# Merging own and former scores into one row of 128 keys, and the first batch's scores from whole fp32 parts, in a transformer layer on one core

## The reference, cut to what matters

```python
x = x + attn(layernorm(x), qkv_w, out_w)      # 16 heads of 16, rotary on q and k, scale 16**-0.5
x = x + ffn(layernorm(x), w1, w2, h1, h2, w3) # silu(w1 x) * (w2 x), gelu(h1 .), gelu(h2 .), w3; hidden 1024

def block_mask(seq_len):                      # which key j a query i sees
    blk = i // 64 == j // 64
    glob = (i < 4) | (j < 4)
    slide = abs(i - j) <= 128
    return (blk | glob | slide) & (j <= i)
```

## Time and profile before

| | |
|---|---|
| median of 3 runs (lowest, highest) | 1135.43 us (1133.87, 1138.61) |
| the profiled execution's own time | 1138.62 us |
| its span, first to last instruction | 1136.8 us |
| TensorE (PE) busy | 1077.8 us, 95% |
| VectorE (DVE) | 638.8 us, 56% |
| ScalarE (ACT) | 717.5 us, 63% |
| GpSimd (POOL) | 473.4 us, 42% |
| mean granted TensorE clock | 0.973 |

### The profile page before, as it was taken

How to read it: one execution, slowest core, us unless ns; L and a number is a source line. 1 busy time by engine, 2 the same in 40 slices (tenths; PEclk the granted TensorE clock), 3 DMA queues, 4 the chain that set the end, 5 groups by cost and what they waited for, 6 DMA issues and landing times.

```text
span 1136.8 us, 21541 instructions
## 1 busy us (share of the span) xinstructions
PE 1077.8 (95%) x7538; PEld 887.7 (78%) x7538; DVE 638.8 (56%) x1986; ACT 717.5 (63%) x1774; POOL 473.4 (42%) x656
## 2 busy tenths in 40 slices
PE   4676899999999999999999999999999999999997
PEld 2455787879778897888878797788978888888886
DVE  4586457555665465654575556654656544555312
ACT  2555458585586576685585865865766855966422
...
GB/s 377 315 167 222 259 206 221 287 146 120 182 223 148 160 184 131 242 84 203 165 167 188 151 119 176 227 145 165 179 130 225 84 201 167 122 103 70 173 128 20
DMA packets 120380, 198.53 MB, mean 175 GB/s; under 512 B 7632, under 2 KB 71376, under 8 KB 119248
## 3 DMA queue, kind: packets, MB, share of 16 engines
...
q10 hardware_dynamic: 1152, 11.53, 2.6%
...
## 4 chain that ended last, share of the span: by engine, by line
PE 78%; ACT 9%; DVE 5%; POOL 3%; issue 3%; DMA 1%; SPq 0%; POOLq 0%; ACTq 0%; DVEq 0%
PE bank L731 35%; PE bank L701 11%; PE bank L755 4%; PE bank L592 4%; PE bank L635 4%; PE bank L529 4%; PE bank L604 3%; PE bank L612 3%; ACT Sm L887 3%; PE bank L557 2%; PE bank L660 2%; POOL a_lo L1370 2%; DVE Sm L1101 2%; ACT L907 2%; ACT a_hi L908 2%
## 5 line engine op out<-in xcount | busy, mean ns | idle before, releaser
L887 ACT ACTIVATE Sm<-Sm,smin 128x260 f32<-128x260 f32 (+2 forms) x512 | 241.4, 473 | 174.5 <-DVE smin L1101 173.9
L731 PE MATMUL bank<-b_hi,W 128*128 128x512 f32 x512 | 214.1, 418 | 0.2 <-POOL b_lo L1370 0.2
L731 PE MATMUL bank<-a_hi,W 128*128 128x512 f32 x512 | 208.1, 406 | 0.1
L731 PE MATMUL bank<-b_lo,W 128*128 128x512 f32 x512 | 201.4, 393 | 0.0
L731 PE MATMUL bank<-a_lo,W 128*128 128x512 f32 x512 | 200.9, 392 | 0.0
L1120 DVE COPY PT<-bank 128x512 f32<-128x512 f32 x128 | 87.9, 687 | 129.5 <-PE bank L635 120.6
L701 PE MATMUL bank<-x_hi,W 128*128 128x256 f32 x512 | 124.9, 286 | 0.0
L701 PE MATMUL bank<-x_lo,W 128*128 128x256 f32 x512 | 123.4, 283 | 0.0
L1379 POOL TENSOR_TENSOR a_lo<-a_act,a_hi 128x256 fp32r<-128x256 f32 x128 | 94.3, 740 | 61.8 <-ACT a_hi L952 61.7
L1370 POOL TENSOR_TENSOR a_lo<-a_act,a_hi 128x512 fp32r<-128x512 f32 x64 | 81.0, 1291 | 82.0 <-ACT a_hi L908 82.0
L1101 DVE CUSTOM_DVE_ANT_0 Sm<-bank,msk,gmin 128x256 f32<-128x256 f32 x256 | 108.3, 479 | 8.0 <-PE bank L592 8.0
...
## 6 DMA issues: line engine op xcount, KB each, us to landing
...
Qs<-qk_scratch SPq DMA_DIRECT2D x128, 128.0 KB, 4.4
...
```

The lines of the kernel that those rows point to most:

```text
L731: mm = nc.tensor.matmul(bank[n % 2][:, :], lhsT.bitcast(F32) if general else lhsT, rhs, start=(kk == 0 and part == 0), stop=(kk == NH - 1 ...
L887: ex = nc.scalar.activation(row, row, ACT.Exp, bias=smin[:, r, c:c + 1], scale=-1.0, accum_out=rowsum[:, i % 2, col:col + 1])
```

## The change

**Merged row.** For tiles 1 to 3 a predicated copy on VectorE writes the former tile's score over the own tile's wherever the own key is masked, in PSUM, two heads at a time. Minimum, exponentials, and turning then run over one row of 128. `turn_prev` and bank 4's separate role go: banks 4 and 5 take turns by unit. After the turn, VectorE keeps the own side by a product with `turned_cur`; ScalarE copies the whole, now after VectorE has (`prev_copied`), and GpSimd multiplies the copy with `turned_prev` (`mask_prev`). Both products with v stay.

**The key 128 back.** In column r own and former key collide. Its score comes from an elementwise product of q with k one tile before (`products_back`, GpSimd) and a matmul with the head mask, six in `global_scores`; it stands as a fifth column beside the keys 0 to 3 (MORE = 5, COLS = 133). After the exponential GpSimd weighs v of the former tile with it (`weigh_back`), and PE adds it turned with a matmul by the identity. The keys 0 to 3 now come from `Gs` for tile 1 too, so `place_global`, `pack_global`, `turn_globals` and the product with `Vg` run for three tiles instead of two.

**First batch.** Batch 0's scores use q and k whole in fp32 (`q_first`, `k_first`) with queries masked by head on GpSimd (`q_masks`), not the stacks: no splitting, no trip through DRAM. The sine product of batch 0's rotary moves from GpSimd to VectorE. The later weights are loaded from SyncE's queue ahead of the opening's steps, eight weight saves are issued at step 8, and `global_scores` and `values_of_first` of batch 0 come before units 2 and 3.

```diff
-COLS = KEYS + NGLOB
+MORE = NGLOB + 1
...
-                for i in range(2):
+                for i in range(NT - 1):
                     for f in range(NF):
                         col = (i * NF + f) * HPT * NGLOB
-                        mm = nc.tensor.matmul(MISC[:, col:col + HPT * NGLOB], q[:, f, (i + 2) * P:(i + 3) * P],
-                                              Kg[:, f, :, :].rearrange("p h j -> p (h j)"), start=True, stop=True)
+                        nc.tensor.matmul(MISC[:, col:col + HPT * NGLOB], q_of(b)[:, f, (i + 1) * P:(i + 2) * P],
+                                         Kg[:, f, :, :].rearrange("p h j -> p (h j)"), start=True, stop=True)
+                pe.wait_ge(back_done, b + 1)
+                for i in range(NT - 1):
+                    for f in range(NF):
+                        col = (NT - 1) * HEADS * NGLOB + (i * NF + f) * HPT
+                        mm = nc.tensor.matmul(MISC[:, col:col + HPT], back_qk[:, f, i * P:(i + 1) * P], headmask,
+                                              start=True, stop=True)
                 mm.then_inc(g_done, 1)
...
                     for c2 in range(2):
                         pair = g * UH // 2 + c2
-                        mm = nc.tensor.matmul(bank[2 + half][:, c2 * KEYS + lo:(c2 + 1) * KEYS],
-                                              Qs[:, pair, half, :],
-                                              Ks[:, pair, i * P + lo - P:(i + 1) * P], start=True, stop=True)
+                        keys = slice(i * P + lo - P, (i + 1) * P)
+                        if a:
+                            lhsT, rhs = Qs[:, pair, half, :], Ks[:, pair, keys]
+                        else:
+                            lhsT, rhs = q_masks[:, n % MASKED_RING, 2 * c2 + half, :], k_first[:, g // 2, keys]
+                        mm = nc.tensor.matmul(bank[2 + half][:, c2 * KEYS + lo:(c2 + 1) * KEYS], lhsT, rhs,
+                                              start=True, stop=True)
                     mm.then_inc(s_done, 1)
-            def turn_cur(a, n):
...
+                    pe.wait_ge(v_kept, 2 * NT * (a + 1))
                 else:
-                    pe.wait_ge(v_kept, 2 * NT * (a + 1))
+                    pe.wait_ge(cur_kept, UNITS * a + n - 1)
+                    if n - 2 >= GROUPS:
+                        pe.wait_ge(prev_copied, LATER * a + n - 2 - GROUPS + 1)
                 for c in range(UH):
-                    mm = nc.tensor.transpose(bank[5][:, c * P:(c + 1) * P], unit_scores(n, P)[:, c, :], ident)
-                mm.then_inc(cur_turned, 1)
-            def turn_prev(a, n):
-                if n < GROUPS:
-                    return
-                wait(pe, prev_kept, LATER * a + n - GROUPS)
-                for c in range(UH):
-                    mm = nc.tensor.transpose(bank[4][:, c * P:(c + 1) * P], Sm[:, n % SM_RING, c, 0:P], ident)
-                mm.then_inc(prev_turned, 1)
+                    mm = nc.tensor.transpose(bank[4 + n % 2][:, c * P:(c + 1) * P], unit_scores(n)[:, c, :], ident)
+                mm.then_inc(turned, 1)
             def turn_globals(r, i):
...
+                    if i:
+                        pe.wait_ge(back_weighed, LATER * a + GROUPS * i)
+                        for f in range(NF):
+                            nc.tensor.matmul(bank[7][:, f * P:(f + 1) * P],
+                                             back_pv[:, i % 2, f, :, :, :].rearrange("p c u d -> p (c u d)"), ident,
+                                             start=False, stop=False, skip_group_check=True)
...
-                act.wait_ge(prev_turned, LATER * a + n - GROUPS + 1)
+                act.wait_ge(cur_kept, UNITS * a + n + 1)
                 wait(act, pv_done, UNITS * a + n - 1)
-                nc.scalar.copy(PT[:, n % 2, 0, :, :].rearrange("p c q -> p (c q)"), bank[4][:, :])\
-                    .then_inc(prev_kept, 1)
+                nc.scalar.copy(PT[:, n % 2, 0, :, :].rearrange("p c q -> p (c q)"), bank[4 + n % 2][:, :])\
+                    .then_inc(prev_copied, 1)
...
+                if i:
+                    for half in range(2):
+                        dve.wait_ge(s_done, HALVES * a + 2 * n + half + 1)
+                        sides = bank[2 + half][:, :].rearrange("p (c s k) -> p c s k", c=2, s=2)
+                        nc.vector.copy_predicated(sides[:, :, 1, :],
+                                                  own_mask.bitcast(U32).unsqueeze(1).broadcast_to([P, 2, P]),
+                                                  sides[:, :, 0, :]).then_inc(merged, 1)
                 for half in range(2):
-                    dve.wait_ge(s_done, HALVES * a + 2 * n + half + 1)
+                    if i:
+                        dve.wait_ge(merged, 2 * (LATER * a + n - GROUPS) + half + 1)
+                    else:
+                        dve.wait_ge(s_done, HALVES * a + 2 * n + half + 1)
                     for c2 in range(2):
                         c = 2 * c2 + half
                         h = g * UH + c
                         tt = nc.vector.tensor_tensor_reduce(
-                            out=unit_scores(n, lo)[:, c, :], in0=bank[2 + half][:, c2 * KEYS + lo:(c2 + 1) * KEYS],
-                            in1=msk[:, int(i == 1), lo:KEYS], scale=1.0,
-                            scalar=gmin[:, i - 2, h:h + 1] if i > 1 else FAR_OFF,
+                            out=unit_scores(n)[:, c, :], in0=bank[2 + half][:, c2 * KEYS + P:(c2 + 1) * KEYS],
+                            in1=merged_mask[i == 1] if i else own_mask, scale=1.0,
+                            scalar=gmin[:, i - 1, h:h + 1] if i else FAR_OFF,
                             op0=ALU.add, op1=ALU.min, accum_out=smin[:, r, c:c + 1])
                     tt.then_inc(s_free, 1)
...
-                nc.vector.tensor_copy(PT[:, n % 2, 1, :, :].rearrange("p c q -> p (c q)"), bank[5][:, :])\
+                nc.vector.tensor_tensor(PT[:, n % 2, 1, :, :], bank[4 + n % 2][:, :].rearrange("p (c q) -> p c q", q=P),
+                                        turned_cur.unsqueeze(1).broadcast_to([P, UH, P]), ALU.mult)\
                     .then_inc(cur_kept, 1)
...
+            def mask_queries(n):
+                i, g = n // GROUPS, n % GROUPS
+                pool.wait_ge(rope_done, 2 * (g // 2) + 1)
+                if n >= MASKED_RING:
+                    pool.wait_ge(s_done, 2 * (n - MASKED_RING) + 2)
+                nc.gpsimd.tensor_tensor(
+                    q_masks[:, n % MASKED_RING, :, :], q_first[:, g // 2, i * P:(i + 1) * P].unsqueeze(1).broadcast_to([P, UH, P]),
+                    headmask[:, g % 2 * UH:(g % 2 + 1) * UH].unsqueeze(2).broadcast_to([P, UH, P]), ALU.mult)\
+                    .then_inc(q_masked, 1)
...
+            def weigh_back(a, n):
+                i, g = n // GROUPS, n % GROUPS
+                if n == GROUPS:
+                    pool.wait_ge(v_kept, 2 * NT * (a + 1))
+                if g == 0:
+                    wait(pool, pv_done, UNITS * a + (2 * GROUPS if i == 3 else 0))
+                values = (v_even, v_odd)[g % 2][:, i - 1, :].rearrange("p (f c u d) -> p f c u d", f=NF, u=2, d=HD)
+                nc.gpsimd.tensor_tensor(back_pv[:, i % 2, g // 2, :, g % 2, :], values[:, g // 2, :, g % 2, :],
+                                        unit_scores(n, P + NGLOB, COLS).broadcast_to([P, UH, HD]), ALU.mult)\
+                    .then_inc(back_weighed, 1)
+            def mask_prev(a, n):
+                pool.wait_ge(prev_copied, LATER * a + n - GROUPS + 1)
+                if a == 0 and n == GROUPS:
+                    pool.wait_ge(masks_made, 3)
+                side = PT[:, n % 2, 0, :, :]
+                nc.gpsimd.tensor_tensor(side, side, turned_prev[:, :].unsqueeze(1).broadcast_to([P, UH, P]), ALU.mult)\
+                    .then_inc(prev_kept, 1)
+            def products_back(b):
+                pool.wait_ge(rope_done, 2 * NF * (b + 1))
+                wait(pool, g_done, b)
+                nc.gpsimd.tensor_tensor(back_qk[:, :, :], q_of(b)[:, :, P:SEQ], k_of(b)[:, :, 0:SEQ - P], ALU.mult)\
+                    .then_inc(back_done, 1)
             def ln2(a, i):
                 rsqrt(a, i, mv2, ve2, rstd2, mv2_done, ve2_done, rstd2_done)
...
+                    if with_q and nq == KG_STEP:
+                        products_back(b)
                     if with_a:
-                        if 2 * GROUPS <= n + 1 < UNITS:
+                        if GROUPS <= n + 1 < UNITS:
                             place_global(a, n + 1)
+                        if GROUPS <= n - T_LAG < UNITS:
+                            mask_prev(a, n - T_LAG)
                         if (i := tile_at(n, 5)) is not None:
...
-                    if with_a and 2 * GROUPS <= n - 1 < UNITS:
+                    if with_a and GROUPS <= n - 1 < UNITS:
                         pack_global(a, n - 1)
+                        weigh_back(a, n - 1)
```

344 lines of the change are left out of this document (192 added, 152 removed).

## The result

The changed kernel takes 1207.18 us (median of 4, 1203.86 to 1207.79), the kernel before beside it 1134.65 (median of 4, 1133.77 to 1138.61): 1.0616 times, 95% interval 1.0592 to 1.0641. That is 72.5 us slower, far outside the range of 1116 to 1162 us. The profiled execution took 1207.79 us around a span of 1206.0.

What follows compares the result with a forecast made beforehand. The prediction took PE to bound the kernel from the first gated tile on, and latency before it. 1138.62 us plus 21.6 behind the opening minus 11 in it gave 1149.2, or 1146 at the median; range 1116 to 1162.

Steps and rivals of the forecast that it cites:

- Slots: PE's own work per round: turn_prev removed, small products added, net -1.0 us in rounds 0 to 5.
- Step 8: In each of rounds 0 to 5, PE waits 3.6 us for GpSimd's late last b_lo.
- the 2.3 us of slack and 4.6 of added work: GpSimd in steps 5 to 8: 4.6 us new work against 2.3 us slack makes the last b_lo 2.3 us later.
- Step 9: PE waits 0.5 us more a round at turn_globals of tile 1, for GpSimd's pack_global of unit 7.
- Steps 12 to 15: Round's end: PE waits 0.44 us longer for a_lo and 0.6 for unit 15's masking chain, together 1.0.
- rival (b): Middle rounds: the 3.6 us waits lower PE's clock, 2 to 3 us lost in each of six, 1161 us; chance 0.2.
- The opening: Before the first gated tile: earlier scores against fp32 passes and GpSimd's work, net -11 us, bounds -22 and +5.
- The charge of 19 us for the fp32 passes: Opening: eight fp32 instructions per unit's scores cost about 1.4 us over 12 units and 0.5 over 4, +19.
- the estimate by GpSimd's list: Opening: GpSimd's own work until unit 15's queries are masked, 64 us from about 28, ends at 100 to 105.
- Rival (a): GpSimd keeps up if its added work in steps 5 to 7 stays under 2.3 us: 1117 us; chance 0.2.
- (c): Rival: the opening gives 20 us and the step-8 wait is half: 1126 us; chance 0.07.
- (d): Rival: the opening gives nothing, as fp32 holds PE: 1157 us; chance 0.1.

Runs made afterwards that it cites:

- e1: Changed kernel with VectorE masking the former side straight out of PSUM, without ScalarE's copy and GpSimd's mask_prev: 1142.33 us, 1.0049 times the kernel before.
- e13: Kernel before plus GpSimd's pass over the former side, six small matmuls in global_scores, and ScalarE's copy waiting for VectorE's keep_cur: 1186.84 us.
- e4: Changed kernel without the six matmuls of 8 columns in global_scores, so its output is another: 1184.84 us.
- e6: e1 with the first batch's scores in one F32R pass instead of the fp32 passes, less exact: 1137.48 us.
- e5: e1 with VectorE making Kg ahead of the masks in the opening: 1138.47 us.
- e9: e1 with Kg ahead of the masks, and first scores and small products in one pass, less exact: 1121.68 us, 0.9876 of the kernel before.

## Why the prediction was wrong, step by step

**Slots, forecast -1.0 us a round.** Measured -1.7 by the split above, -1.0 in e1 with the same work on PE. The dropped `turn_prev` gives 0.44 a unit as worked out from the earlier trace rows: units 7 and 8 start 0.47 and 0.93 us sooner within the round. `global_scores` grew from 0.81 to 2.60 us, the forecast 1.8; a `back_pv` pair takes 0.64, not 0.55. Right.

**Step 8, forecast a wait of 3.6 us.** Measured 3.35 + 0.46 = 3.81. The argument from the 2.3 us of slack and 4.6 of added work held; `mask_prev` takes 1.30 us and `weigh_back` 0.30.

**Step 9, forecast 0.5 us at `turn_globals`.** It waits there only in round 6, 0.4 us; in rounds 0 to 5 half clock had made PE late by then.

**Steps 12 to 15, forecast 1.0 us on top of the 1.2 that a round had.** Measured 0.90 + 1.70 + 0.66 + 0.75 = 4.0, 2.9 more than before, and a stretch of half clock there in two rounds. This step failed by what it left out. Its chain of turn, VectorE, ScalarE and GpSimd for unit 15 was put at 0.6 us and measures 0.75. But for the units before it `mask_prev` was followed as work and not as a wait: `mask_prev(11)` holds GpSimd's queue for 4.26 us, the last 3.5 of them with four `a_lo` ready. The trace of before could have told it, for ScalarE's copy of unit 11 stood behind gelu and exponentials there too:

```profile
367.91 0.57 ACT L894 COPY PT<-bank 128x512 f32<-128x512 f32 x1
```

That is 101.3 us into the round, 4.9 after its `turn_prev` began. Nothing on GpSimd waited for it then. The new order, ScalarE behind VectorE, adds to it (1.23 us at unit 10; in e13 11 to 14 us over the run).

**The clock, forecast as rival (b), 0.2, 15 us in six rounds.** This is the term that was sized worst. The chain is the one that (b) named, idle PE and then half clock, and its 2 to 3 us were nearly right for the one place it looked at: 3.4 us in e4, which has only that place. But 5.4 us a round were lost, since behind `global_scores` there was a second drop without idle time in four rounds and near the round's end in two a third; that is 27 us in rounds 1 to 5. e1 shows what depends on it: with the waits cut to 2.2 us a round, 4.7 of the 5.4 us go with them. The argument against (b), that waits of 1 us leave the clock at 1.00, was true and said nothing of waits of 4. By the sign that the prediction gave for it, a clock under 1.00 in the middle rounds, (b) is what happened, at more than twice its price. As a rival (b) should have been joined to the forecast wait of 3.6 us, not set beside it: the forecast carried the cause and left out the effect. The Trainium skill, TensorE: Matmul & The Clock Gate, section HAM oscillation — how this bites in real kernels, has waits that come back between bursts of matmuls throttle PE each time, and the windows at 351 and 355 us (0.59 and 0.56) agree. The drop at 371, with PE busy ahead of it, that section would not have told.

**The opening, forecast -11 us.** Measured +6.6 in this pair of profiles. First scores at 24.52 were right to 0.1 us. The charge of 19 us for the fp32 passes was far too high: one pass gives back 4.9 us of the whole run (e6). What the step left out is the queue of VectorE: 3.5 us of making masks (26.14 to 29.60), two of them short operations at 1.64 and 1.02 us, ahead of `Kg`, and all of `global_scores` at half clock on the path, 5.1 us to the third unit. Moving one call (e5) makes it 6.0 us sooner there and 3.9 us in the end. The two errors had opposite signs, and the second was followed by waits of 5.4 and 3.3 us for `rot` and of 6.1 us for `mask_prev` that the estimate by GpSimd's list did not see. With both mended, and the mask on VectorE, the first gated tile starts at 124.5 (e9), near the forecast's 123.

**Together.** Forecast 21.6 - 11 = 10.6 us, measured 69.2. Of the 58.6 between them, rounds 0 to 5 hold 60.0 - 24.6 = 35.4, of which half clock is 30.6 (3.4 in round 0 and 27.2 in rounds 1 to 5); idle time is 8.6 more than forecast and the slots 3.8 less. The opening holds 6.6 + 11 = 17.6. What follows round 5, forecast at -3.0 and measured at +2.6, holds 5.6: there it is `mask_prev` again, for in round 6 PE idles 5.2 us against 1.1 in e1, and the whole stretch is 6.8 us longer than e1's. Rival (a) fell at the point that the prediction gave for it, (c) and (d) concerned mainly the opening and both were too kind.
